# A block of gated scan and routed experts on one core: experts chosen by sorted logits, mean terms on GpSimd, scan products written over the gates, fewer transfers, a third expert buffer, and new orders on every engine

## The reference, cut to what matters

```
h = layernorm(x) * (1 + ca) + sa                   # ca, sa, ga, cb, sb, gb: from a condition, one row each
h = rmsnorm(h) * norm_w
v = h @ W_v.T                                       # 8 heads of 16
gates = softmax((h @ W_a.T) as (8 heads, 16 rows, 17))   # over the 17
state[i] = gates[i, 0] * v[i] + sum_j gates[i, 1 + j] * state_before[j]    # a scan over the 512 tokens
x = x + ga * (h_in + state @ W_out.T)
h = layernorm(x) * (1 + cb) + sb
logits = h @ router_weight.T + router_bias          # 8 experts, the 4 largest kept, softmax over those 4
y = sum over the 4 experts of weight * (down @ ((up + 1) * gate * sigmoid(1.702 * gate)) + bias)
x = x + gb * y
```

## Time and profile before

| | |
|---|---|
| three runs | 786.08, 790.71, 795.59 us (median 790.71) |
| the profiled execution | 789.0 us, its span 787.3 us |
| instructions | 12543 |
| busy | PE 589.9, DVE 678.0, ACT 552.2, POOL 567.5 us |
| mean granted TensorE clock | 0.917 of full speed |
| transfers | 85.34 MB, mean 108 GB/s |

### The profile page before, as it was taken

The page is one execution under the profiler, slowest core; times in us unless marked ns, Lnnn a source line. Parts: engine busy times, 40 slices in busy tenths (PEclk is TensorE's granted clock), DMA queues, the critical chain, the costliest instruction groups (busy, mean ns, idle before and its releaser), DMA issues.

```text
span 787.3 us, 12543 instructions
## 1 busy us (share of the span) xinstructions
PE 589.9 (75%) x2826; PEld 441.0 (56%) x2826; DVE 678.0 (86%) x2921; ACT 552.2 (70%) x1272; POOL 567.5 (72%) x635
## 2 busy tenths in 40 slices
PE   5785144787968697877878686979788785878986
PEld 3242022565746475665657474757666574757875
DVE  4569999999999999999999999999989999888331
ACT  4764142777786878787777878786867776657885
POOL 2685556687878797888878787978878686735554
PEclk9886565899999999999999999998989997889998
DMA  6265645453726455364537273644545463720000
GB/s 189 83 145 139 139 116 137 102 130 83 171 79 149 107 122 120 79 159 81 129 95 160 77 159 97 134 115 116 117 79 122 108 141 86 163 71 8 14 8 7
DMA packets 162234, 85.34 MB, mean 108 GB/s; under 512 B 77752, under 2 KB 156784, under 8 KB 157936
## 3 DMA queue, kind: packets, MB, share of 16 engines
q1 hardware_dynamic: 162160, 84.55, 46.3%
HBM read 44.66 MB, written 39.85 MB: 107 GB/s over the span
## 4 chain that ended last, share of the span: by engine, by line
DVE 66%; PE 14%; issue 10%; ACT 5%; POOL 3%; DMA 1%; SPq 1%; POOLq 0%; ACTq 0%; DVEq 0%
DVE ps L854 15%; DVE prod L846 14%; DVE ps L860 8%; DVE act_t L926 7%; DVE nmax L824 6%; DVE zs L831 6%; PE ps L1184 6%; PE ps L1197 4%; DVE rz L837 3%; PE ps L1171 2%; ACT ex L590 1%; ACT ps L624 1%; POOL ex L414 1%; ACT up L618 1%; DMA gates<-gate_dram 1%
## 5 line engine op out<-in xcount | busy, mean ns | idle before, releaser
L1184 PE MATMUL ps<-h2t,wgu 128*128 128x256 f32 x1024 | 256.4, 393 | 24.6 <-ACT up L618 24.6
L1184 PEld LDWEIGHTS ps<-h2t,wgu 128*128 128x128 f32 x1024 | 192.6, 196 | 71.4 <-ACT up L618 29.8
L1171 PE MATMUL ps<-wl,ht 128*128 128x512 f32 (+1 forms) x320 | 168.4, 629 | 71.5 <-ACT lg L601 67.6
L1197 PE MATMUL ps<-wd,act_t 128*128 128x128 f32 x1024 | 146.5, 288 | 65.7 <-DVE act_t L926 65.6
L1197 PEld LDWEIGHTS ps<-wd,act_t 128*128 128x128 f32 x1024 | 135.3, 200 | 95.4 <-DVE act_t L926 84.9
L854 DVE TENSOR_REDUCE ps<-prod 128x8 f32<-128x136 f32 x512 | 152.5, 298 | 10.6
L846 DVE TENSOR_TENSOR prod<-gates,ps 128x136 f32<-128x136 f32 x512 | 147.1, 287 | 14.7 <-DMA gates<-gate_dram 6.4
L421 POOL TENSOR_TENSOR lg<-lg,nmax 128x1088 f32<-128x1088 f32 x64 | 130.3, 2039 | 15.0 <-DVE nmax L824 13.1
L676 ACT ACTIVATE weighted<-ps,comb 128x128 f32<-128x128 f32 x256 | 79.9, 363 | 85.4 <-PE ps L1197 83.1
L461 POOL TENSOR_SCALAR up<-up 128x512 f32<-128x512 f32 x128 | 78.4, 612 | 79.3 <-ACT up L618 75.2
L414 POOL TENSOR_TENSOR ex<-ex,rz 128x1088 f32<-128x1088 f32 x64 | 129.2, 2039 | 8.8 <-DVE rz L837 5.7
(11 more groups left out here) (122 smaller groups left out, 586.0 us busy)
## 6 DMA issues: line engine op xcount, KB each, us to landing
gate_dram<-ex SPq DMA_DIRECT2D x256, 136.0 KB, 3.3
gates<-gate_dram SPq DMA_DIRECT2D x32, 1088.0 KB, 5.5
yt_tok<-y_dram SPq DMA_DIRECT2D x256, 8.0 KB, 3.4
xg<-in_L_attn_x_dram SPq DMA_DIRECT2D x32, 64.0 KB
y_dram<-ys SPq DMA_DIRECT2D x32, 64.0 KB, 2.0
out_dram<-res_out SPq DMA_DIRECT2D x32, 64.0 KB
wa_rows<-in_L_attn_W_a_dram SPq DMA_DIRECT2D x1, 1088.0 KB, 5.7
dn_rows<-in_L_ffn_down_proj_dram SPq DMA_DIRECT2D x1, 1024.0 KB, 12.3
```

The costliest lines, as they stand in the source:

```text
L1171: nc.tensor.matmul(ps[:, n % 2, 0:w], ht[:, g % RH, j * P:(j + 1) * P], wl[:, k * LC:k * LC + w], start=True, stop=True).then_inc(lg_ps.se ...
L1184: last = nc.tensor.matmul(gu_ps(m, k, which)[:, q * N:(q + 1) * N], wgu[:, k, rows + q * P:rows + (q + 1) * P], h2t[:, m % 2, :], start=Tr ...
L1197: last = nc.tensor.matmul(dn_ps(j), act_t[:, k % 2, q * N + j * P:q * N + (j + 1) * P], wd[:, k, q, :], start=(q == 0), stop=(q == KI - 1))
```

## The change

It has six parts.

1. Products over the gates: `scan_products` multiplies 16 of each 17 gates by the 16 states and writes the result over the gates; the state loses its constant 1, and `prod` is gone. `scan_sums` sums the 17 values of each row in `gates`.
2. `mean_term` moves from VectorE (one instruction) to GpSimd (two, with a wait between).
3. Experts by sorted logits: the 8 largest logits in order (`max`, a tile at a time), the last four of these overwritten with 2^127, then `match_replace` marks the places of the first four; the mask `lower` and the pairwise comparisons are gone.
4. `store_gates` and `load_y` issue four transfers per tile in place of eight, each twice the size.
5. `up`, `act_t` and `weighted` get three buffers, and the waits of `up_and_silu` and `weigh_expert` move back by one expert.
6. New orders in the `run` of GpSimd, ScalarE and TensorE, and new slots in `between`.

```diff
@@ sync
-                for b in range(B):
-                    sp.dma_start(gate_dram[j, b // 2, :, b % 2].rearrange("r t e -> t r e"),
-                                 ex[b * TS:(b + 1) * TS, j, :].rearrange("p (r e) -> p r e", e=ROW)
+                for q in range(B // 2):
+                    sp.dma_start(gate_dram[j, q].rearrange("r b t e -> (b t) r e"),
+                                 ex[2 * TS * q:2 * TS * (q + 1), j, :].rearrange("p (r e) -> p r e", e=ROW)
                                  ).then_inc(g_st[j].sem, 16)
...
@@ gpsimd
+            def mean_term(mv, rs, rs_ok, nm, nx_ok, nm_ok, c):
+                pool.wait_ge(rs_ok.sem, rs_ok.at(c, 1))
+                nc.gpsimd.tensor_tensor(nm[:, :, 0], mv[:, :, 0], rs[:, :, 0], ALU.mult).then_inc(nx_ok.sem, 1)
+                pool.wait_ge(nx_ok.sem, nx_ok.at(c, 1))
+                nc.gpsimd.tensor_scalar(nm[:, :, 0], nm[:, :, 0], -1.0, 0.0, ALU.mult, ALU.add).then_inc(nm_ok.sem, 1)
...
@@ scalar, up_and_silu (weigh_expert alike, with acc_ok)
-                if k >= 2:
-                    act.wait_ge(act_ok.sem, act_ok.at(m, k - 1))
-                elif not is_first(m):
-                    act.wait_ge(act_ok.sem, act_ok.at(m - 1, E + k - 1))
+                if m * E + k >= NB:
+                    act.wait_ge(act_ok.sem, act_ok.at(m, k + 1 - NB))
@@ vector
-                nc.vector.tensor_tensor(
-                    prod[:, :].rearrange("p (i k) -> p i k", k=M1),
-                    gates[:, t, :].rearrange("p (i k) -> p i k", k=M1),
-                    state[:, (t - 1) % TS, :].unsqueeze(1).broadcast_to([P, HALF, M1]), ALU.mult).then_inc(scan.sem, 1)
+                own = gates[:, t, :].rearrange("p (i k) -> p i k", k=M1)[:, :, 1:M1]
+                nc.vector.tensor_tensor(own, own, state[:, (t - 1) % TS, :].unsqueeze(1).broadcast_to([P, HALF, M]),
+                                        ALU.mult).then_inc(scan.sem, 1)
...
-                    nc.vector.tensor_tensor(rl_ps, logit, bias, ALU.add).then_inc(rank_in.sem, 1)
                 elif n == 1:
...
-                    nc.vector.tensor_tensor(req, other, own, ALU.is_equal).then_inc(rank_in.sem, 1)
+                    for j in range(TILES):
+                        nc.vector.max(top[:, j, :], rl[:, j, :]).then_inc(rank_in.sem, 1)
                 elif n == 2:
...
+                    nc.vector.memset(top[:, :, TOP_K:E], BIG).then_inc(rank_in.sem, 1)
                 else:
-                    dve.wait_ge(rank_in.sem, rank_in.at(p, 7))
-                    nc.vector.tensor_tensor(rgt[:, :, :, :], rgt[:, :, :, :], req, ALU.add).then_inc(rank_in.sem, 1)
+                    dve.wait_ge(rank_in.sem, rank_in.at(p, 5))
+                    for j in range(TILES):
+                        nc.vector.match_replace(out=left[:, j, :], in_to_replace=top[:, j, :], in_values=rl[:, j, :],
+                                                imm_value=-BIG).then_inc(rank_in.sem, 1)
...
```

More of the change, by code:

```diff
@@ L225, in adaln_block @@
         norm_ok = event("norm_ok", 2 * TILES)
-        g_st = [event(f"g_st{j}", 16 * B) for j in range(TILES)]
+        g_st = [event(f"g_st{j}", 16 * B // 2) for j in range(TILES)]
         g_ld = [event(f"g_ld{j}", 16) for j in range(TILES)]
@@ L475, in run @@
             def run(a, g, e, s, p, m, o):
+                if o is not None:
+                    finish(o)
+                if m is not None:
+                    clamp_up(m, 0)
+                    clamp_up(m, 1)
+                if e is not None:
+                    gate_value(e, 0)
                 if a is not None:
@@ L1044, in between @@
                             aggregate(st2, mv2, st2_ok, mv2_ok, p, j)
+                elif u == 64:
+                    if m is not None:
+                        hidden(m, 4)
                 elif u == 66:
@@ L1258, in run @@
             def run(a, g, e, s, p, m, o):
-                if g is not None:
-                    logits(g, 0)
                 if m is not None:
@@ L1263, in run @@
                 if g is not None:
+                    logits(g, 0)
                     logits(g, 1)
@@ L1277, in run @@
                     gate_up(m, 2)
+                    down(m, 1)
                 if g is not None:
-                    logits(g, 5)
-                if m is not None:
-                    down(m, 1)
+                    logits(g, 4)
                 if p is not None:
@@ L1286, in run @@
                 if g is not None:
-                    logits(g, 6)
+                    logits(g, 5)
                 if p is not None:
@@ L1294, in run @@
                 if g is not None:
-                    logits(g, 8)
+                    logits(g, 7)
                 if m is not None:
                     gate_up(m, 4)
+                    down(m, 3)
                 if g is not None:
+                    logits(g, 8)
                     logits(g, 9)
+                if m is not None:
+                    gate_up(m, 5)
                 if a is not None:
@@ L1302, in run @@
                 if m is not None:
-                    down(m, 3)
-                    gate_up(m, 5)
                     down(m, 4)
```

338 lines of the change are left out of this document (145 added, 193 removed).

## The result

| | before | changed |
|---|---|---|
| device time, median (us) | 793.15 (786.08 to 797.34, four runs) | 801.88 (800.14 to 804.10, four runs) |
| ratio | | 1.0147, 95% interval 1.0096 to 1.0199 |
| span of the profiled execution (us) | 787.3 | 800.6 |
| mean granted TensorE clock | 0.917 | 0.892 |

The change makes the kernel 1.5% slower. Forecast were 774 us and a range up to 792: the range misses.

A forecast was written before the change was run, and what follows sets the result against it. VectorE, busy 86% of the span, was taken as the bound. Eleven passes gave 11.9 us, passes around them 3.0, the start 2.5: 17.4, less 2.5 for the clock, 14.9 off 789.0, so 774, range 763 to 792.

The forecast's parts named there:

- the part on sorted logits: Expert choice on VectorE: five 128 x 128 instructions gone save 0.58 us, new ones cost 0.2, net 0.38 a pass.
- rival 4: Expert choice on VectorE: match-and-replace takes 0.56 us apiece, costing 2.5 us a pass; kernel at 802 us; chance 3%.
- the allowance of 2.5 us for the clock: TensorE at a granted clock of 0.96 loses 1.7 us, exceeding a slack of 1.0 by 0.7, in some four passes.
- Products: Scan products on VectorE: 128 elements in place of 136, 0.009 us less each, 0.28 us a full pass.
- Mean terms: Moving them from VectorE to GpSimd saves 0.36 us at slot 69 and 0.07 at slot 12, 0.43 a pass.
- New rank instructions: Two maxima, a memset and two match-and-replace on VectorE, about 0.16 us each, costing near 0.2 us a pass.
- Third buffer: Expert buffers of ScalarE and GpSimd: the wait of `up_and_silu` was already met, so gain and loss 0.
- Four transfers: SP's gate issues: hidden in full passes; before the first product 0.9 us saved, between 0 and 3.1.
- Table loads: ScalarE: two more in each of 13 passes at 1.28 us, 2.6 us a pass, hidden in idle time.
- rival 1: Table loads on ScalarE don't hide: 805 us if none is covered, chance 8%; some 790, no change, another 8%.
- VectorE waits for ScalarE in every pass: Sign in the profile after that would prove the forecast wrong, pointing to table loads that don't hide.
- rank instructions dear: Sign that would prove the forecast wrong: passes still last 42.9 us with VectorE busy 41.

The follow-up runs named there:

- a_rdl_psum: Changed kernel with the router's logits also written to PSUM, where `rdl` alone reads them: 788.95 us, 0.9946 of the kernel before.
- a_fill8: Changed kernel, inputs still in SBUF, with eight unread matmuls in TensorE's idle stretch ahead of `down(m, 0)`: 791.29 us, 1.0001 of the kernel before.
- b_fill6: Kernel before the change with six unread matmuls in TensorE's gap of 2.74 us: 785.85 us, 0.9923 of the kernel before.
- a_psum_fill8: Changed kernel with router logits and selected exponentials in PSUM, plus eight unread matmuls ahead of `down(m, 0)`: 772.10 us, 0.9744 of the kernel before.
- c_three_oldorder: Changed kernel with the old orders and slots, and router logits, selected exponentials and marked logits in PSUM: 775.43 us, 0.9779 of the kernel before.
- a_psum_exp1_first: Changed kernel with router logits and selected exponentials in PSUM, second exponential moved back ahead of `up_and_silu(m, 0)`: 775.57 us, 0.9785 of the kernel before.
- a_psum_oldorder: Changed kernel with router logits and selected exponentials in PSUM, and the old orders and slots: 789.78 us, 0.9993 of the kernel before.
- a_psum_fill4: Changed kernel with router logits and selected exponentials in PSUM, plus four unread matmuls ahead of `down(m, 0)`: 776.20 us, 0.9822 of the kernel before.

## Why the prediction was wrong

**The step that failed first** stands in the part on sorted logits: it costs the five new instructions from both sides and lets the old ones keep their price. `rdl` was in both kernels, so it got no line in the sum. But the change moves its input from PSUM to SBUF, and that made it 1.5 us on average. The prediction had the fitting row in hand: the mean term of 0.56 in the earlier trace rows. It was read as a size (a short instruction that happens to be long) and used as the far end for match-and-replace, 2.5 us a pass, rival 4 with 3% and 802 us. That rival's time was met within 0.2 us by luck, since the mechanism is another: match-and-replace takes 0.15. A look at what ran beside the 0.56 (the clamp, 0.61) and at the same line at 0.16 would have shown a wait rather than a size. Price: 13 us in the changed kernel (a_rdl_psum), 19 with the clock kept up.

**The second** is the allowance of 2.5 us for the clock. It took the granted clock as a loss spread evenly over a pass (0.04 x 42.9) that hits some slack, in four passes. The runs show a fall of TensorE to its lower level for some 7 us behind one certain gap, in each full pass, and the new order itself made that gap: I laid its ScalarE part against VectorE's slots slot by slot, and never TensorE's idle stretches. Price: 11 us in the changed kernel (a_fill8), 17 with the holds gone; some 6 of that the kernel before pays too (b_fill6).

**Point by point.** *Products*: 0.28 forecast, 0.19 measured alone. *Mean terms*: 0.43 forecast, 0.39 measured. *New rank instructions*: 0.15, 0.15 and 0.08, at the level I took. *Third buffer*: not run alone; nothing in the traces speaks for or against its 0. *Four transfers*: none in a pass, as forecast; before the first product 0.9 of the 2.8 us of issues arrives by the landing times, the 0.9 that was taken, but the start of the first product lies anywhere from 55.6 to 58.1 in the traces with the old orders and from 52.5 to 57.4 in those with the new, so the forecast 55.6 against 55.87 is no proof of the terms. *Table loads*: 26 more at 1.28, and hidden (at most 0.15 of 2.6 us a pass); rival 1 was rightly doubted. *Drain*: 57.6 against 58.4, forecast no change. *The first two passes*: 37.58 and 38.13 against 37.97 and 38.71, 0.39 and 0.58 less, forecast 0.3 and 0.9. *The whole*: with both causes out (a_psum_fill8) passes last 42.01 and the kernel takes 772.1; c_three_oldorder has passes of 41.87. The forecast was 41.8, and 771.6 ahead of the allowance. That 772.1 comes so near is in part luck: the forecast started from an execution of 789.0 with two passes of 44.34 in it. Against the kernel before with its clock kept up (b_fill6, 785.85) a_psum_fill8 gains 13.8 us, where 17.4 were forecast, and a quiet pass 0.98 us (41.87 against 42.85), where 1.1 were. So the gains were nearly as large as read; two costs were missed.

**The signs.** The text named "VectorE waits for ScalarE in every pass" and "rank instructions dear" as what would prove it wrong. The first didn't come: from 131 to 668 us VectorE waits longest for GpSimd's `xn`, 5.6 us in 11 waits. The second came by its sign (long passes, VectorE busy over 41), not by its cause. A held instruction counts as busy time and shows in no list of waits.

## What to carry to other kernels

When an edit moves a tensor between SBUF and PSUM, price the instructions that read it as well, the unchanged ones first: look for VectorE instructions with both inputs in SBUF that are far longer than their size, and at what GpSimd does at that moment. Such a hold is busy time, not a wait; keep one of the two inputs in PSUM.

When an order changes, list TensorE's idle stretches of one pass before and after, not its sum: the durations behind them, the longest first, tell whether the clock fell. If it did, put real work into the stretch (or a few unread matmuls, as a test); the same matmuls elsewhere only cost.

Two limits that hide each other give small gains one by one (13 and 11 us) and the whole only together (30 us); a fix that gives half of what it should is not yet a refutation.

## What the runs showed of the hardware

- A short VectorE instruction with two SBUF inputs that starts while a GpSimd tensor instruction runs ends 0.01 to 0.04 us after it: 1.93 us behind one of 2.04, 0.56 behind one of 0.61, for 16 and 2 elements. With one input in PSUM it takes 0.17 in the same place, and one that started 0.06 ahead of GpSimd's took 0.16. I hadn't expected a wait of one engine for another that no semaphore asks for.
- After 3.90 us of idle time TensorE takes 2.08 for what takes 1.05 to 1.16 at the full clock, in every full pass; filled up, the granted clock is 1.00. Behind a gap of 2.74 it falls in some passes and not in others, in the same program, and it fell behind gaps of 1.60 and 1.77 with others close before them (a_psum_exp1_first, a_psum_oldorder).
- Those passes can alternate strictly (41.87 and 43.54 in c_three_oldorder, 42.09 and 43.26 in a_psum_fill4) though each does the same work. What picks them is open.
- Four issues of SP with twice the bytes took 3.50 us, eight took 6.26: the time goes mostly, not wholly, by the number.
